# One core's attention and expert block: query turning moved ahead of the token lists, row one-hots moved from VectorE to ScalarE

## What is computed

```python
xn = layernorm(x)
q, k, v = (xn @ W + b for each)            # 16 heads of 16
q, k = rope(q), rope(k)                    # pairs of columns turned by the position's angle
attn = softmax(causal(q k^T / 4)) v @ Wo + bo
p = softmax(xn @ gate^T)                   # 64 experts
w, ids = top_k(p, 6); w = w / sum(w)
routed = sum_e w_e * down_e(silu(g_e) * u_e)      # 176 hidden
shared = down_s(silu(g_s) * u_s)                  # 352 hidden
out = x + attn + routed + shared
```

## Time and profile before

| | us |
|---|---|
| median of 3 runs | 649.49 (647.65 to 653.19) |
| the profiled execution | 650.96 |
| its span, first to last instruction | 649.1 |
| TensorE busy | 615.3 (95%) |
| VectorE busy | 430.5 (66%) |
| GpSimd busy | 321.0 (49%) |
| ScalarE busy | 307.2 (47%) |

### The profile page before, as it was taken

The page is one execution under the profiler, slowest core; times in us unless marked ns, Lnnn a source line. Parts: engine busy times, 40 slices in busy tenths (PEclk is TensorE's granted clock), DMA queues, the critical chain, the costliest instruction groups (busy, mean ns, idle before and its releaser), DMA issues.

```text
span 649.1 us, 17796 instructions
## 1 busy us (share of the span) xinstructions
PE 615.3 (95%) x4929; PEld 364.3 (56%) x4929; DVE 430.5 (66%) x1366; ACT 307.2 (47%) x802; POOL 321.0 (49%) x340
## 2 busy tenths in 40 slices
PE   6999999998998999998999999999999899999987
PEld 3644455654554555554555555555554566666654
DVE  6768688557664665667665565544446788899865
ACT  3643131033443444444444544444445777777752
POOL 4000000268636775567765686564300776766662
PEclk9999999999997999999999999999999999999999
DMA  9610011138978768996799977996425777777432
GB/s 297 179 30 2 0 34 34 57 103 255 283 228 278 232 190 247 320 334 185 213 298 295 315 222 235 327 327 134 102 59 193 210 232 229 227 227 232 129 109 74
DMA packets 78167, 124.52 MB, mean 192 GB/s; under 512 B 11113, under 2 KB 52618, under 8 KB 78090
## 3 DMA queue, kind: packets, MB, share of 16 engines
q1 hardware_dynamic: 43098, 60.18, 30.4%
q0 software_dynamic: 15872, 46.16, 24.4%
q10 hardware_dynamic: 19120, 17.18, 7.8%
HBM read 85.73 MB, written 37.75 MB: 190 GB/s over the span
## 4 chain that ended last, share of the span: by engine, by line
PE 80%; DVE 6%; DMA 3%; issue 3%; ACT 3%; POOL 2%; DVEq 1%; SPq 0%; ACTq 0%; POOLq 0%
PE pair L1216 23%; PE pair L1243 14%; PE pair L1186 6%; PE pair L1173 5%; PE pair L1121 4%; PE bank L1227 4%; PE bank L1330 4%; PE bank L1200 3%; PE bank L1362 2%; PE pair L1083 2%; DVE negm L985 2%; DMA lower<-xn_rows,idx_all 2%; PE pair L1292 2%; PE pair L1312 1%; PE bank L1341 1%
## 5 line engine op out<-in xcount | busy, mean ns | idle before, releaser
L454 POOL DMA_INDIRECT lower<-xn_rows,idx_all x128 | 138.0, 1078 | 221.8 <-DVE idx_all L958 107.8
L1216 PE MATMUL pair<-space,work 128*64 (+1 forms) x768 | 167.4, 467 | 6.3 <-DVE wqkv_sb L932 3.7
L1243 PE MATMUL pair<-lower,work 88*64 x512 | 121.5, 379 | 0.7 <-ACT lower L615 0.7
L1216 PEld LDWEIGHTS pair<-space,work 128*64 128x64 f32 x768 | 67.4, 138 | 78.4 <-issue 66.9
L874 DVE TENSOR_TENSOR work<-work,pair 128x176 f32<-128x176 f32 x128 | 42.9, 337 | 101.5 <-ACT work L609 100.7
L1243 PEld LDWEIGHTS pair<-lower,work 88*64 88x64 f32 x512 | 69.6, 137 | 48.7 <-issue 18.0
L1216 PE MATMUL pair<-wqkv_sb,work 128*64 128x352 f32 x256 | 90.6, 477 | 0.0
L615 ACT ACTIVATE lower<-pair 128x256 f32<-128x256 f32 x128 | 49.1, 384 | 76.5 <-PE pair L1243 76.5
L519 POOL DMA_INDIRECT wqkv_sb<-y_rows,slot_i x48 | 48.1, 1002 | 58.2 <-DVE negm L985 33.2
L602 ACT ACTIVATE work<-pair 128x256 f32<-128x256 f32 x128 | 42.6, 381 | 66.9 <-PE pair L1173 41.3
L985 DVE TENSOR_REDUCE negm<-pair 128x2 f32<-128x256 f32 (+1 forms) x128 | 64.6, 549 | 9.5 <-PE pair L1292 7.5
(11 more groups left out here) (205 smaller groups left out, 1156.5 us busy)
## 6 DMA issues: line engine op xcount, KB each, us to landing
space<-wgu SPq DMA_DIRECT2D x66, 352.0 KB
y_rows<-lower ACTq DMA_DIRECT2D x128, 128.0 KB, 4.3
qk_all<-qk_rows SPq DMA_DIRECT2D x64, 256.0 KB
lower<-wdn SPq DMA_DIRECT2D x64, 176.0 KB
qk_rows<-qk_all POOLq DMA_DIRECT2D x32, 256.0 KB, 5.7
qk_rows<-space POOLq DMA_DIRECT2D x16, 256.0 KB, 4.0
xn_rows<-qk_all SPq DMA_DIRECT2D x16, 128.0 KB, 1.9
lower<-xn_rows,idx_all POOLq DMA_INDIRECT x128
```

The source lines that it names most:

```text
L454: po.indirect_dma_start(xg[:, r % XB, :], None, xn_rows[:, :], bass.IndirectOffsetOnAxis(idx_all[:, r:r + 1], 0)).then_inc(xg_in[r % XB], 16)
L1216: last = pe.matmul(pair[u % 2][strip, 0:2 * F], xgT[u][:, c, strip], n, start=c == 0, stop=c == EC - 1, skip_group_check=True)
L1243: last = pe.matmul(pair[u % 2][strip, 512:512 + E], hT[:, u % 2, c, strip], n, start=c == 0, stop=c == 1, skip_group_check=True)
```

## The change

GpSimd turns and stores the queries (pieces 0, 2, 4, 6) before it waits for the lists. Each piece waits for its own span's projections, piece 2 also for the routing tables, since its buffer lies over routing data. Behind the gathers there remain the stores of the keys, one behind each odd gather: those of span s begin at the first odd r of at least 18 (s + 1) + 12. `gS` moves into `wqkv_sb`, so that `spare[0]` is free.

The row one-hots go to ScalarE: behind the silu of a beat it makes, for each tile listed at that beat, six distances |number - row| and then max(0, 1 - distance) over all six. VectorE negates `slot_row` once for it and makes `is_tile` alone. `list_tokens` waits for both.

```diff
--- before.py
+++ after.py
@@ -241,10 +241,10 @@
         hT = work[0:FP, :, EC * P:(EC + 2) * P].rearrange("p u (k q) -> p u k q", q=P)
         hS = [[z[:, at * SPAN_T:(at + 1) * SPAN_T] for at in range(2)] + [work[:, u, EC * P:EC * P + SPAN_T]]
               for u, z in enumerate((y.rearrange("p u e -> p (u e)"), freed[0]))]
-        gS = [raw[:].rearrange("p u s -> p (u s)"), on[:].rearrange("p s e -> p (s e)")]
         sg, hid = work[:, :, 4 * P:4 * P + F], work[:, :, 6 * P:6 * P + F]
 
         wqkv_flat = wqkv_sb[:].rearrange("p c n -> p (c n)")
+        gS = [wqkv_flat[:, u * SPAN_T:(u + 1) * SPAN_T] for u in range(2)]
         own_gu = [wqkv_flat[:, 0:GU].rearrange("p (c n) -> p c n", c=EC),
                   room[:, 1, 0:GU].rearrange("p (c n) -> p c n", c=EC)]
         own_dn = [wqkv_flat[0:FP, GU:GU + DN].rearrange("p (c n) -> p c n", c=2), room[0:FP, 1, GU:GU + DN].rearrange("p (c n) -> p c n", c=2)]
@@ -274,7 +274,7 @@
         dchain = sem("dchain")
         exp_in = sem("exp_in"); exp_ok = sem("exp_ok"); chosen = sem("chosen"); counted = sem("counted")
         tiled = sem("tiled"); placed = sem("placed"); passed_ok = sem("passed_ok"); ended = sem("ended")
-        tables_ok = sem("tables_ok"); onehot_ok = sem("onehot_ok"); listed = sem("listed"); idx_ok = sem("idx_ok"); dpair = sem("dpair")
+        tables_ok = sem("tables_ok"); rows_set = sem("rows_set"); away_ok = sem("away_ok"); row_hot = sem("row_hot"); onehot_ok = sem("onehot_ok"); listed = sem("listed"); idx_ok = sem("idx_ok"); dpair = sem("dpair")
 
         w_loaded = [sem("w_loaded_even"), sem("w_loaded_odd")]
         gu_own = sem("gu_own"); dn_own = sem("dn_own"); idx_col = sem("idx_col"); po_turn = sem("po_turn"); roped = sem("roped"); turned_ok = sem("turned_ok");
@@ -469,8 +469,10 @@
                 if n or k:
                     po.wait_ge(roped, ROPE_STEPS * (n // 2) + k)
                     po.sem_inc(po_turn, 1)
-                if n == 0 and k == 0:
-                    po.wait_ge(sdn_ok, NT)
+                if k == 0:
+                    po.wait_ge(qkv_ok, 4 * g + 2)
+                if n == 2 and k == 0:
+                    po.wait_ge(tables_ok, 1)
                 if k == 0 and n >= BUFS:
                     po.wait_ge(rows_out[u], 16 * 2 * COPIES * (n // BUFS))
                 cos, sin = (table[:, a, cs].unsqueeze(1).to_broadcast([P, SPAN_T // S, S]) for cs in range(2))
@@ -492,19 +494,20 @@
                     i = po.tensor_tensor(q[:, k - 7], q[:, k - 7], other[:, k - 7], ALU.subtract)
                 i.then_inc(roped, 1)
 
-            po.wait_ge(qkv_ok, len(order))
             po.wait_ge(tables_in, 1)
+            po.wait_ge(xn_out, 16 * NT)
+            for n in range(0, PIECES, 2):
+                for k in range(PIECE_STEPS):
+                    piece(n, k)
             po.wait_ge(idx_ok, 1)
-            po.wait_ge(xn_out, 16 * NT)
-            steps = [(n, k) for n in range(PIECES) for k in range(ROPE_STEPS if n % 2 else 0, PIECE_STEPS)]
-            todo = len(steps)
+            steps = [(n, k) for n in range(1, PIECES, 2) for k in range(ROPE_STEPS, PIECE_STEPS)]
             done = 0
             for r in range(RT):
                 gather(r)
-                while r >= XB and r % 2 and done < (r - XB + 1) * todo // (RT - 4 * XB) and done < todo:
+                if done < len(steps) and r % 2 and r >= 2 * ROPE_STEPS * (steps[done][0] // 2 + 1) + 3 * XB:
                     piece(*steps[done])
                     done += 1
-            assert done == todo
+            assert done == len(steps)
 
             def rows(t, u):
 
@@ -646,8 +649,27 @@
                 rows = ROWS[k % CHUNKS]
                 act.activation(gS[k % 2][0:rows], pair[k % 2][0:rows, 0:SPAN_T], ACT.Silu).then_inc(ssilu_ok, 1)
 
-            for k in range(BEATS):
-                shared_silu(k)
+            def hot_rows(t):
+
+                u = t % 2
+                if t == 0:
+                    act.wait_ge(rows_set, 1)
+                    act.wait_ge(pad_ok, 1)
+                    act.wait_ge(consts_b, 1)
+                if t >= 2:
+                    act.wait_ge(listed, t - 1)
+                for k in range(TOPK):
+                    last = act.activation(is_row[:, u, k], iota_b[:], ACT.Abs, bias=slot_row[:, t, k:k + 1])
+                last.then_inc(away_ok, 1)
+                act.wait_ge(away_ok, t + 1)
+                act.activation(is_row[:, u], is_row[:, u], ACT.Relu, bias=v_all[:, 0, 0, D:D + 1], scale=-1.0).then_inc(row_hot, 1)
+
+            for k in range(BEATS + 1):
+                if k < BEATS:
+                    shared_silu(k)
+                for t in range(NT):
+                    if LIST_AT[t] == k:
+                        hot_rows(t)
                 if k == MASKS_AT:
                     half_masks()
             for i in range(XB):
@@ -826,6 +848,8 @@
             link(dve.tensor_scalar(part_i[:], slot_i[:], SHIFT, None, ALU.arith_shift_right))
             link(dve.tensor_copy(slot_tile[:], part_i[:]))
 
+            dve.tensor_scalar(slot_row[:], slot_row[:], -1.0, None, ALU.mult).then_inc(rows_set, 1)
+
             dve.memset(last_tf[:, 0:SHARED], float(STRIPS))
             dve.memset(tile_ef[:, :, TILES:TILES + 2 * XB], float(XT - 1))
             dve.wait_ge(ended, 1)
@@ -846,7 +870,6 @@
                 if t >= 2:
                     dve.wait_ge(listed, t - 1)
                 for k in range(TOPK):
-                    dve.tensor_scalar(is_row[:, u, k], iota_b[:], slot_row[:, t, k:k + 1], None, ALU.is_equal)
                     last = dve.tensor_scalar(is_tile[:, u, k], iota_b[:], slot_tile[:, t, k:k + 1], tok_sb[:, t:t + 1],
                                              ALU.is_equal, ALU.mult)
                 last.then_inc(onehot_ok, 1)
@@ -1151,6 +1174,7 @@
 
             def list_tokens(t):
                 pe.wait_ge(onehot_ok, t + 1)
+                pe.wait_ge(row_hot, t + 1)
                 for k in range(TOPK):
                     mm = pe.matmul(listed_at, is_row[:, t % 2, k], is_tile[:, t % 2, k], start=t == 0 and k == 0,
                                    stop=t == NT - 1 and k == TOPK - 1, skip_group_check=True)
```

## The result

| | before | after |
|---|---|---|
| median, run side by side | 650.95 us (4 runs) | 657.46 us (4 runs, 656.72 to 658.58) |
| ratio, 95% interval | | 1.0125 [1.0091, 1.0158] |
| span of the profiled execution | 649.1 | 654.7 |

The forecast was 668 us and +18.4 on the profiled execution; on the spans it is +5.6 (the two medians alone give a ratio of 1.010, inside the interval). Where the 5.6 us come from, first by stage. These are the windows of the changed kernel that answer to the earlier trace rows, with their limits moved to where the stages end now (columns as there: PE, PEld, DVE, ACT, POOL, granted clock, DMA share, GB/s).

A forecast was written before the change was run, and what follows sets the result against it. TensorE fills the projections and list stage; only the expert stage has holes, 17.4 us. Terms -15.5 + 1 + 19.6 + 5.5 + 3 + 4.8 = +18.4 on 650.96: 669.4, by the median 668 us; range 648 to 690.

The forecast's parts named there:

- The turning moved forward, +5.5: Routing: GpSimd's products hold VectorE's eight `run_b` sums, so TensorE waits 5.5 us for `chosen`; bounds 0 to +7.
- signs named for being right: TensorE idle before most lists behind `Relu`, idle near 46 us, `run_b` sums over 1 us, expert stage some 15 us shorter.
- the idle stretch near 46 us: Sign in the routing: TensorE idle behind `run_b`, where it wants `chosen` at 45.71 us.
- `is_tile` held, +3: List stage: GpSimd's 27 turning operations may hold VectorE's 96 tile one-hots; +3 us, between 0 and +10.
- Clock, +4.8: TensorE's clock falls twice, behind the 5.5 us wait and at tile 7, 2.4 us each; bounds 0 and +35.
- ScalarE's one-hots, +19.6: List stage: ScalarE takes 2.83 us a tile and TensorE's lists wait for it; +19.6 us, some +6 to +26.
- Expert stage, -15.5 + 1: Of 17.4 us lost in holes, 15.5 go with GpSimd's wait and turning; +1 for a buffer reused by later keys.
- The buffer meeting: Expert stage: span 2's keys reuse span 0's buffer, span 3 likewise; a late store delays VectorE; +1 us, 0 to +5.
- The part for the keys: Expert stage: GpSimd's 7.86 us wait for VectorE's turned keys, with gathers behind it, loses 5.9 us, which go.
- The part for the turning: Expert stage: GpSimd's turning products hold VectorE, delay weight copies and stand between gathers; 9.6 us counted, which go.
- Rival A: Short sums and one-hots are not held, clock stays at full speed: 656 us, by the median 654.6; chance 0.13.

The follow-up runs named there:

- ahead_halves: ahead with each of GpSimd's 36 turning operations cut into two of 256 columns and a wait between them; 641.03 us, 0.9894 of before.
- no_turn: The changed kernel with none of GpSimd's 36 turning operations, unturned queries stored; 655.00 us, 1.0082 of before.
- hots_only: The kernel before with the row one-hots on ScalarE and nothing else of the change; 667.81 us, 1.0264 of before.
- ahead: The changed kernel with ScalarE's row one-hots made one beat earlier; 649.42 us, 0.9984 of before.
- keys_late: The kernel before with only the key stores moved behind later gathers, as in the change; 644.45 us, 0.9923 of before.
- first_ahead: keys_late with the queries of span 0 alone turned and stored ahead of the lists; 637.44 us, 0.9812 of before.

## Why the forecast was wrong, step by step

- **The turning moved forward, +5.5: failed.** The step was "if each waits out a GpSimd operation and goes in the gap behind it with its own 0.2, the eighth ends at 51.2". The hold is real and a whole operation long, but a gap lets two through: eight sums need four gaps, 4 x 1.45 = 5.8 us, and end 0.3 us before TensorE wants them. Measured +0.3. Of the signs named for being right, three came, and the idle stretch near 46 us did not. ahead_halves shows that the gaps set it, and no_turn that the products do the holding. The Trainium skill ("SBUF — State Buffer", Who interferes with whom) says that the engine without the port pair blocks fully for the other's whole instruction. The trace agrees (1.19 us against 0.19) for every second one; the others pass in the gap, and on them the term hung.
- **`is_tile` held, +3: failed by the same step.** Six take 6 x 0.705 = 4.2 us (8.46 for twelve), not 8.9, which is less than ScalarE's pace leaves. Measured 0: hots_only has the same list stage. Had ScalarE been in time, the holds would have cost 9.6 us of waits (ahead).
- **Clock, +4.8: too large.** Two falls of 2.4 were taken; the first hung on the wait of 5.5 that did not come, the second came at tile 7 as expected and cost 1.6.
- **ScalarE's one-hots, +19.6: right, the sum in part by luck.** 2.83 us a tile was 2.81. The waits were 1.77, 0.45, 0.93, 1.38 and 1.91 where 1.89, 0.77, 1.28, 1.55 and 1.9 were expected. They come to 17.7, a tenth less, and 2.0 that no term foresaw, for rows that no longer overlap at the waits, bring it to 19.7. No row gave the 0.07 for the semaphore: here 0.15 us pass from the end of `Relu` (70.86) to the list (71.01).
- **Expert stage, -15.5 + 1: right in size, -16.0.** The buffer meeting did not come. The part for the keys was right (keys_late). The part for the turning was counted for all 36 operations as one; first_ahead shows that 27 of them could have stayed among the gathers for about 1 us (from the list stage to the end it takes 500.6 us, the changed kernel 499.4), spaced as they are there.
- **The sum.** 18.4 - 5.2 (sums) - 3 (one-hots) - 3.2 (clock) - 1.5 (expert stage) + 0.1 (lists) = 5.6. Rival A, whose condition was that short operations are not held, came to 656 on the profiled execution, close to what was measured, but for another reason: they are held and lie beside other work.

## What to carry to other kernels

When an engine is held up by another one's operations, count what passes in one gap before multiplying: a short operation behind a held one may pass free. Two costs that fall on different engines in front of the same wait don't add: price each alone, and take the later one. Before work is moved out of a stage because it disturbs it, try it there in another order: here the better kernel moved a quarter of the turning to where it has cover, and left the rest behind the gathers, singly and at a slower pace. And where the profile names who ended a wait, look in the program for what the waiting step needs.

## What the runs showed of the hardware

While GpSimd ran products of 512 columns back to back (1.27 us, gap 0.18), VectorE passed two operations per product, sums of two 16-bit inputs (0.19 us alone) and `tensor_scalar` one-hots (0.30 alone) alike: one stood 1.2 to 1.4 us, one was not held. With GpSimd's operations halved, the held ones stood 0.60 to 0.86 us. At a place in the expert stage a cast and a copy behind it (0.69 and 0.52 us when not held) were each held by a half, for 1.1 us together, as long as the cast alone was by a whole product. TensorE's granted clock fell in one execution and not in another with the same waits in front of the same matmuls.
